# Spreading a side stream over an attention trunk: one quantised-FFN step in every trunk step from 16 to 95, in place of four in five from 16 to 115

## What is computed

```
x = x + L0_xattn(ctx, layernorm(x), ctx)      # 16 heads of 64, causal
x = x + L0_ffn(layernorm(x))                  # silu(gate) * up, then down, 352 wide;
                                              # inputs, weights and h in blockwise FP4
x = x + L1_xattn(layernorm(x), ctx)           # two softmaxes: keys 0..76 and 77..127
x = x + L1_ffn(layernorm(x))                  # top-2 of 8 experts, 512 wide
```

## The kernel before, in words

| phase | PE | ACT | DVE |
|---|---|---|---|
| 0 | transpose fx (L424) | high half (L691) | c: exponent, magic, round; a: low half |
| 1 | | | c: back, scaled (L869 silu_h); n: row sums, centre |
| 2 | transpose h (L414) | n: mean square (L671); c: four copies of hT (L698, L700) | |
| 3 | down (L430) | | n: scale (L908 fx), max, inverse, divide (L848); c: add to x |
| 4 | gate (L443 to L445) | c: mean square (L671 fy); a: tanh (L707) | n: exponent, magic, round; c: row sums, centre, scale (L908 fy); a: product (L1003) |
| 5 | transpose fy (L452) | high half (L677) | n: back, scaled; c: low half (L912) |
| 6 | up | | a: h (L1010) |
| 7 | | | a: max, inverse, divide (L848 q_xn) |

## Time and profile before

### The profile page before, as it was taken

One profiled execution on the slowest core, in us unless ns is written; L12 is line 12 of the kernel. 1 busy time (PEld: TensorE's weight loads), 2 busy tenths in 40 slices (PEclk: granted clock), 3 DMA queues, 4 the chain that ended last, 5 costly groups with the idle time before them and its releaser, 6 DMA issues.

```text
span 707.5 us, 16586 instructions
## 1 busy us (share of the span) xinstructions
PE 634.3 (90%) x5849; PEld 577.9 (82%) x5849; DVE 534.1 (75%) x1454; ACT 439.1 (62%) x1121; POOL 306.8 (43%) x428
## 2 busy tenths in 40 slices
PE   3879999989898999999999999999999987879980
PEld 2768888878787888999999988889888976879980
DVE  7796677788898888888899896888665474566655
ACT  3568787878777876555656556565664345456760
POOL 3134444344434343353444343445236655467660
PEclk9999999999999999999999999999999799999995
DMA  9600000000000000326664050000000002122215
GB/s 232 217 1 1 1 3 1 1 3 1 1 2 2 1 17 2 120 55 126 122 119 91 1 150 2 1 2 1 2 5 28 28 20 54 46 54 66 68 53 182
DMA packets 49389, 33.27 MB, mean 47 GB/s; under 512 B 9414, under 2 KB 45868, under 8 KB 49308
## 3 DMA queue, kind: packets, MB, share of 16 engines
q1 hardware_dynamic: 47036, 27.55, 16.4%
q0 software_dynamic: 2272, 4.67, 2.0%
HBM read 17.57 MB, written 14.63 MB: 46 GB/s over the span
## 4 chain that ended last, share of the span: by engine, by line
PE 49%; DVE 17%; issue 14%; ACT 8%; POOL 7%; DMA 2%; SPq 1%; DVEq 0%; POOLq 0%; ACTq 0%
PE ps_j L402 6%; PE ph L1442 5%; PE ps_s L557 5%; PE py L1453 5%; ACT scores L770 4%; PE ps_h L629 4%; DVE scores L1029 4%; PE ps_t L593 4%; PE ps_j L364 4%; PE ps_h L608 3%; POOL probs L1282 3%; PE ps_j L366 3%; PE ps_j L365 3%; DVE neg_max L1036 3%; POOL xs_scratch L1372 3%
## 5 line engine op out<-in xcount | busy, mean ns | idle before, releaser
L1282 POOL TENSOR_TENSOR probs<-scores,rsums 128x308 f32<-128x308 f32 (+1 forms) x192 | 153.6, 814 | 228.1 <-DVE rsums L1049 227.8
L1044 DVE TENSOR_REDUCE sums<-scores 128x4 f32<-128x308 f32 (+1 forms) x192 | 90.8, 501 | 42.6 <-ACT scores L770 34.9
L593 PE MATMUL ps_t<-ident,probs 128*128 128x128 f32 x512 | 79.6, 279 | 22.2 <-ACT probsT L784 17.4
L770 ACT ACTIVATE scores<-scores,neg_max 128x128 f32<-128x128 f32 x256 | 81.6, 393 | 17.9 <-DVE neg_max L1036 17.4
L657 ACT ACTIVATE QT<-ps_j 128x512 f32<-128x512 f32 x64 | 38.3, 598 | 83.1 <-PE ps_j L366 83.1
L593 PEld LDWEIGHTS ps_t<-ident,probs 128*128 128x128 f32 x512 | 58.6, 142 | 29.0 <-issue 22.2
L784 ACT ACTIVATE probsT<-ps_t 128x512 f32<-128x512 f32 x128 | 75.3, 589 | 7.8 <-PE ps_t L593 7.6
L557 PE MATMUL ps_s<-KT,QT 64*128 64x128 f32 x1024 | 77.1, 292 | 0.8 <-ACT KT L663 0.8
L557 PEld LDWEIGHTS ps_s<-KT,QT 64*128 64x128 f32 x1024 | 64.6, 194 | 9.6 <-issue 3.3
L608 PE MATMUL ps_h<-probsT,V 128*64 128x128 f32 x1024 | 70.0, 279 | 0.8 <-DVE x_sb L815 0.8
L629 PE MATMUL ps_h<-Wo,headsT 128*128 128x128 f32 x512 | 69.9, 280 | 0.0
(11 more groups left out here) (239 smaller groups left out, 1621.0 us busy)
## 6 DMA issues: line engine op xcount, KB each, us to landing
xs_scratch<-xs SPq DMA_DIRECT2D x8, 1032.0 KB, 8.2
xt<-xs_scratch SPq DMA_DIRECT2D x39, 64.5 KB, 1.8
w1b<-in_L_ffn_w_dram SPq DMA_DIRECT2D x1, 2048.0 KB, 9.4
big_raw<-in_L_ffn_w_dram SPq DMA_DIRECT2D x8, 256.0 KB, 4.7
ysum<-y_scratch SPq DMA_DIRECT2D x4, 512.0 KB, 5.5
x_sb<-in_x_dram SPq DMA_DIRECT2D x4, 256.0 KB, 3.8
ctx_sb<-in_ctx_dram SPq DMA_DIRECT2D x4, 256.0 KB, 4.7
Wo<-in_L_xattn_Wo_dram SPq DMA_DIRECT2D x2, 512.0 KB, 6.6
```

Of the source, the lines that this page charges most:

```text
L593: ins = nc.tensor.transpose(ps_pT[:, j * S:(j + 1) * S], probs[s % 2][:, j, :], ident[:, :])
L770: ins = nc.scalar.activation(scores[s % 4][:, j, :], scores[s % 4][:, j, :], ACT.Exp, bias=neg_max[:, s % 4, 0, j:j + 1])
L1044: ins = nc.vector.tensor_reduce(sums[:, p4, i, :], scores[p4][:, :, k0:k1], AX_X, ALU.add)
L1282: ins = nc.gpsimd.tensor_tensor(probs[(s - 1) % 2][:, :, k0:k1], scores[r][:, :, k0:k1], rsums[:, r, i, :].rearrange("p (h a) -> p h a", a ...
```

## The change

`ffn_at` gives one FFN step for every trunk step from 16 (`FFN_FROM`) to 95 (`FFN_TO` is now (8 + 4) * 8 = 96): u = N - 16. 48 of the 80 steps fall in the first attention layer, 32 in the second, and trunk steps 96 to 115 have none. Phase and trunk step have the same number within a group, so phases 0, 2, 4, 6 are always in even trunk steps; before, phases 0, 1, 3 and 6 were in even ones and 2, 4, 5 and 7 in odd ones. `D_AT` of the first three groups moves with it; the other groups' times stay.

```diff
-        FFN_FROM, FFN_TO = 2 * STEPS, (NG - 1) * STEPS - 4
-
-        D_AT = [(81, 83, 84, 85), (91, 93, 94, 95), (101, 103, 104, 105), (106, 107, 108, 109), (111, 112, 113, 114),
+        FFN_FROM, FFN_TO = 2 * STEPS, (GROUPS + 4) * STEPS
+
+        D_AT = [(84, 85, 86, 87), (92, 93, 94, 95), (100, 101, 102, 103), (106, 107, 108, 109), (111, 112, 113, 114),
                 (116, 117, 118, 119), (124, 125, 126, 127), (NG * STEPS + 4,)]
@@
             if FFN_FROM <= N < FFN_TO:
-                u, before = (N - FFN_FROM) * 4 // 5, (N - FFN_FROM - 1) * 4 // 5
-                if u == before:
-                    return idle
+                u = N - FFN_FROM
                 F = u // STEPS
                 return {"s": u % STEPS, "n": F if F < GROUPS else None, "a": F - 1 if 0 <= F - 1 < GROUPS else None,
                         "c": F - 2 if 0 <= F - 2 < GROUPS else None}
```

## The result

| | before | after |
|---|---|---|
| median of 4 runs, us | 710.98 (709.70 to 716.53) | 737.41 (736.60 to 740.83) |
| profiled execution, us | 709.29 | 740.83 |
| its span, us | 707.5 | 739.1 |
| PE / DVE / ACT / POOL busy, us | 634.3 / 534.1 / 439.1 / 306.8 | 647.1 / 550.5 / 436.2 / 310.1 |

The changed kernel is slower, by a ratio of 1.0362 with the interval 1.0305 to 1.0418. I had forecast 718.4 us and a range up to 723: the sign was right, and the size was about a third of what came (8.7 us over the median of before, where 26.4 came).

The account below looks back on a forecast made before the run. It took the first layer as bound by a loop through DVE's and ACT's queues, the second by PE's own work. First layer + 12.3 and second layer - 3.2 on 709.3 gave 718.4 us, range 711.5 to 723.

Parts of the forecast that it names:

- The loop through the queues in the first layer: First layer: a chain through DVE's and ACT's queues ends each pair of trunk steps; 36.15 us a full rotation.
- 0 1: First-layer trunk-step pair with FFN phases 0 and 1: set by DVE, 8.7 us plus 0.65 for a collision, 9.35 forecast.
- 2 3: First-layer pair with phases 2 and 3: hT copies between ACT's exponentials, 8.0 us plus 0.5 for a collision, 8.5 forecast.
- 4 5: First-layer pair with phases 4 and 5: ACT's mean square waits for DVE's centring and delays the exponential; 10.8 us.
- 6 7: First-layer pair with phases 6 and 7: taken over unchanged from the old schedule at 7.45 us.
- Rotations 0 and 1: First layer's thin first rotations, with only group n, then n and a: 27.5 and 29.1 us.
- what leaves is 5.4: Second layer: one rotation of FFN matmuls and an up projection leave PE, 5.4 us less, at most 6.5 with tails.
- The stall in "4 5": Second layer: the late exponential costs 0.7 us in each of three pairs, 2.2 in all with group D's steps.
- Rival C: Second layer stalls in full in three "4 5" pairs, 5.1 us for 2.2, total 721.3; chance 0.13.
- The last ten pairs: Second layer's end, without FFN: PE full and the stretch shorter by 6.6 to 7 us.
- Rival A: DVE and POOL miss each other: rotation 35.0 us, first layer + 7.7, total 713.8; chance 0.25.
- Rival B: Denser steps are free: first-layer rotation falls to DVE's own 31.3 us, 7.2 less, total 698.9; chance 0.07.

Follow-up runs that it names:

- Moving the split away: Changed kernel with POOL's split of the second layer's weights in steps 4 and 5 of each first-layer group instead of 1 and 3: 731.18 us, ratio 1.0259.
- the other parity: Changed kernel with the whole FFN one trunk step later, even phases in odd trunk steps: 728.75 us, ratio 1.0236.
- the fillers: Changed kernel with 7 and 11 empty matmuls before phases 3 and 5 in the first layer: 734.09 us, ratio 1.0294; with 10 and 18: 737.73 us.

## Why the prediction was wrong, step by step

- **The loop through the queues in the first layer** was right. "0 1", "2 3", "4 5", "6 7" at full clock are 9.84, 8.13, 10.87 and 7.47 us, together 36.31, for 36.15 forecast. The exponential's delay (5.65 for 5.6) and L867 beside probs (1.53 for 1.5) are as told. That the sum came so near is in part luck, since two misses of opposite sign met in it: "0 1" half a microsecond over 9.35 by the cast, "2 3" 0.4 under 8.5.
- **"'6 7' had this form already: 7.45"** is the step that failed most. It took for granted that PE runs at full clock in a schedule whose PE waits are twice as long. Five stretches at half clock cost 8.0 us of the 13.0 by which the first layer missed 201.2. The prediction had computed that the chain delays PE, and never asked what PE does while it waits. In the earlier trace rows PE is busy 38.02 of 41.10 us; in the rotation after it is 32.3 of 37.9.
- **Rotations 0 and 1** were put at 27.5 and 29.1, and took 29.4 and 31.0. Each has one "2 3" of 8.94, where L906 on fx, now one step behind its rstd with POOL's probs beside it, takes 1.25 for the 0.42 of the earlier trace rows, and the small L840 and L846 behind it are held too. I had allowed 0.2 for a collision. Moving the split away gives back 1.0 of each. Together 3.8 us. The remaining 1.3 of the 13.0 are the full rotations: +0.16 each and a last "6 7" of 8.1 without half clock.
- **The second layer**: "what leaves is 5.4" was right, to 0.1. The stall in "4 5" was the mis-sized term: 0.7 three times, 2.2 in all, and it measured 7.1. On PE the four "4 5" pairs take 11.21, 11.21, 11.02 and 10.27, against some 9.5 of own work: about 1.7, 1.7, 1.5 and 0.8, together 5.7. The windows above say the same: from step 64 to 115 PE is idle 6.7 us in the changed kernel and 1.0 in the one with the sparse second layer. The other 1.4 are in PE's busy time, 224.5 for 223.1, whose ends are modelled; their cause is open. The count was wrong too: there are four such pairs, one in each of rotations 6 to 9, and I took three. Rival C had 1.7 each, and was right on the size of one stall. I argued against it with "PE without a gap now", but that gap-free PE was a PE fed by the old schedule. The place of the wait was also another: not the scores behind a late exponential, but the transposes of fy behind the product and the scaling, as PE's waits in 299.3 to 449.5 show (total, times, longest):

```profile
PE pf L450 <- DVE silu_h L1001: 3.8, 3, 1.3
PE pf L450 <- DVE fy L906: 1.2, 1, 1.2
```

- **The last ten pairs** with PE full and shorter by 6.6 to 7: 81.0 for 88.1, PE busy 80.29. Right.
- **Rival A** (no collisions) fell: in a full rotation L867, L901, L840 and L846 are 0.64, 0.52, 0.82 and 0.73 us longer beside POOL's work, 2.7 together, where I took 1.15. How much of it reached the marks is shown only for the cast and L1301, by moving them. **Rival B** (denser is free) fell with the sign. Behind it stood the Trainium skill's page Perfetto Trace Analysis, section "Optimization Strategy", which says that interleaving stretches with different limits may gain. Here it lost: the stretch that received the work is bound by neither engine's busy time but by a chain across four. The same section goes on to ask for the gaps on the engine and the semaphore behind each. In the new profile that leads to PE's gaps of 2.80 and 1.93 us, and with both filled the clock no longer fell there.
- **The range** ended at 723, and its upper end was built from the bounds of single terms of a mechanism that I had. The cases in which the list of mechanisms is short of one had no room in it.

## What to carry to other kernels

Where a schedule across in-order engines is made denser, add up the chain of each period through all its engines, and then look at what the longest chain does to the waits of TensorE. Waits like those of 1.9 and 2.8 us here are a cost twice, by itself and by the clock of the matmuls behind it. That an engine is full in the old profile does not show that it has slack to take up a later chain. And cut the profile by period: a mean clock of 0.96 over a layer is a pair of 9.0 us beside one of 7.5.

## What the hardware showed that I had not expected

- **Half clock behind waits of 1.9 and 2.8 us in an else busy PE.** From 237.3 to 254.0 PE is busy 13.42 of 16.70 us with waits of 1.93 and 2.80 us, and the last 3.4 us run at 1.2 GHz. The price in the changed kernel is 1.5 to 1.6 us for each, as pairs of the same form at either level show (9.03 and 7.47; 12.5 and 10.87); at the other parity the one stretch cost 0.9 (11.68 and 10.82). Every full rotation has the same waits, but "4 5" was hit in the first, both "4 5" and "6 7" in the second, and "6 7" in the last two. In the kernel with the dense first layer alone, which has the same instructions there, others were hit (171.6, 209.2, 246.7, 274.0). With the fillers the clock fell once behind a wait of 1.81 us (at 136), and in the changed kernel it did not behind the same wait of 1.82. Which wait brings the fall stays open. That filling both takes the falls away between 140 and 300 us is shown.
- **Even a tiny DVE instruction can be held for a whole POOL instruction.** L840 on 128x16 took 0.99 us at 238.16 (0.17 in the kernel before, at 260.12, with POOL idle), and POOL's probs had begun at 238.08:

```profile
238.08 1.04 POOL L1280 TENSOR_TENSOR probs<-scores,rsums 128x512 f32<-128x512 f32 x1 [2.51 <-DVE rsums L1047]
```

The Trainium skill's page SBUF — State Buffer, section "Who interferes with whom", names `tensor_scalar` among the operations that can take the port pair which DVE shares with POOL; the trace agrees with that for this one. I had counted only instructions with two SBUF inputs.
- **A row of POOL instructions holds DVE twice.** Probs from 230.14 and the cast from 231.12 held the scaling (1.53 for 0.89) and then the centring behind it (0.93 for 0.41): DVE got its turn only at the end of each, and the cast in its turn took 1.38 us for 0.72.
